# The eight turns of an attention kernel, written out in a row instead of six in a loop

## The chip, the cores and the metric

The kernel runs on one core of a Trainium2 chip. The metric is the device time of one launch in microseconds (us), as the median of several runs. A core has five engines with an instruction stream each: TensorE (PE in the profile, with its weight loads as PEld), VectorE (DVE), ScalarE (ACT), GpSimd (POOL) and SyncE (SP), which here only issues transfers. They meet through semaphores alone.

## The reference, cut to what matters

```python
x = L0_attn_x_bld                                  # (2, 2048, 256) float32
x = x + attention(layernorm(x))                    # 16 heads of 64, causal, keys and values from a 64-wide latent
x = x + ffn(layernorm(x))                          # 2 rounds: router, top 2 of 6 experts, shared experts, rms norm

# attention, per sequence b and head h
q = x @ Wq[:, h];  latent = x @ Wkv_down           # latent (2048, 64), shared by the heads
k = latent @ Wk_up[:, h];  v = latent @ Wv_up[:, h]
p = softmax(where(causal, q @ k.T / 8, -max))
y += (p @ v) @ Wout[h]
```

## The kernel before, in words

`build` first makes the combined weights, then runs `build_attention` for each of the two sequences in a loop over `b` that all engines execute (line 2238), and then `build_mixture`, the feed-forward part, which is written out in a row and is not touched.

`build_attention` works on pairs of heads: `PAIRS` is 8, and one pair is a **turn**. A turn has `2 * STEPS` = 80 steps, 40 for each head (called `half` in the code). A step is one block of scores: 128 keys (`kt`) against up to 512 queries (`qb`, four blocks of 512). Float32 precision is had by splitting each operand into a high and a low part. In one step:

- PE makes one block of scores of the next head, only to find its row maxima (`max_scores`, line 446), then the block of scores itself (lines 460 and 461), then the product of probabilities and values of five steps before (`use_latents`, lines 480 to 482, `LAG` = 5). Now and then it also projects queries of the next turn (line 426) and transposes a row of maxima (line 436).
- DVE masks a diagonal block (line 737, and 783 for the maxima), reads the maxima (line 786, `read_max`), splits queries (line 731), and at fixed steps inverts the sums of a finished block of queries (`invert`, line 742) and scales the result (`divide`, line 746). Three times per turn it makes a low part in POOL's place (line 363).
- ACT takes the exponential twice, as float32 (line 609, `pr`) and rounded (line 612, `ph`), and copies results out of PSUM (lines 570, 577, 588, 595).
- POOL makes the low parts `pl = pr - ph` (line 363), in a ring of `RING` = 8 buffers, and the low parts of the queries (line 675).
- SP moves the sums of a finished block to 128 partitions (line 379, `sums<-y_sums`), writes the reciprocals out (line 381), reads them back to 64 partitions (line 383) and stores the scaled block (line 388).

The order of the work is written out by hand in each engine's `turn`; no queue or planner chooses at run time. The last steps of a turn's products are done in the first steps of the next turn, so the turns overlap. DVE's `invert` for a block stands eleven steps behind the block's last score or less (`INVERT_AFTER` = 8) and in DVE's own order of instructions, so DVE waits there if the transfer of line 379 has not landed.

What the change touches is `turns` (line 315) and the end of SP's program (lines 407 to 411). Before, turn 0 and turn 7 are written out, and turns 1 to 6 are one body in a loop (`eng.Fori(1, PAIRS - 1)`, line 318) on PE, ACT, POOL and DVE. In that body `p` is a register, so that each wait's target value is computed by a register instruction (FUSED_REGOPS in the trace); in the written-out turns it is a constant. SP has two loops of its own, over turns 1 to 5 and over turns 6 and 7.

Of the kernel before, what the change touches and what calls it, by code (L numbers as in the profile page):

```python
# [38 lines left out]
PAIRS = H // 2  # L39
# [17 lines left out]
def f32(ap):  # L57
    return ap.bitcast(F32)
# [151 lines left out]
def build_attention(nc, T, x_seq, y_seq, recip_rows):  # L210
# [5 lines left out]
    with ExitStack() as ctx:  # L216
# [64 lines left out]
        def project_job(qb):  # L281

            return START_JOBS.index(("proj", qb))
# [30 lines left out]

        def turns(eng, turn):

            turn(0, True, False)
            with eng.Fori(1, PAIRS - 1) as p:
                turn(p, False, False)
            turn(PAIRS - 1, False, True)  # L320

        def block_jobs(job, s, after, p, first):

# [42 lines left out]
        with nc.Block() as block:  # L366
            @block.sync
            def _(sp):
                def stage(pair, projected):
                    if projected is not None:  # L370
                        sp.wait_ge(S["bank_made"], projected)
                    sp.dma_start(f32(stage_hi[:, :, :]), f32(T["m_hi"][:, pair, :, :])).then_inc(S["staged"], DMA)
                    sp.dma_start(f32(stage_lo[:, :, :]), f32(T["m_lo"][:, pair, :, :])).then_inc(S["staged"], DMA)

                def divide(p, half, qb):

                    n = 8 * p + 4 * half + qb
                    sp.wait_ge(S["y_copied"], n + 1)
                    sp.dma_start(sums[:, qb, :], y[LD:LD + 1, qb, :]).then_inc(S["sums_in"], DMA)
                    sp.wait_ge(S["recip"], n + 1)  # L380
                    sp.dma_start(recip_rows[qb], sums[:, qb, :]).then_inc(S["recip_out"], DMA)
                    sp.wait_ge(S["recip_out"], DMA * (n + 1))
                    sp.dma_start(rec[:, qb, :], recip_rows[qb:qb + 1, :, :].rearrange("a p j -> a (p j)").broadcast_to(
                        [LD, BLK])).then_inc(S["recip_in"], DMA)

                def store(p, half, qb):
                    sp.wait_ge(S["normed"], 8 * p + 4 * half + qb + 1)
                    sp.dma_start(y_seq[qb, half * LD:(half + 1) * LD, p, :], y[0:LD, qb, :]).then_inc(S[f"stored{qb}"], DMA)

                def turn(p, more, first=False):  # L390
                    for half in range(2):
                        for qb in range(QB):
                            divide(p, half, qb)
                            if half or qb:
                                store(p, half - (qb == 0), (qb - 1) % QB)
                            elif not first:
                                store(p - 1, 1, QB - 1)
                            if more and (half, qb) == (0, 2):
                                stage(p + 2, FIRST_JOBS + NJOBS * p + 8)

                for g in range(QB):
                    sp.dma_start(x[:, TPB * g:TPB * (g + 1), :],
                                 x_v[:, TPB * g:TPB * (g + 1), :]).then_inc(S[f"loaded{g}"], DMA)
                    if g == 0:
                        stage(0, None)
                stage(1, project_job(QB - 1) + 1)
                turn(0, True, first=True)
                with sp.Fori(1, PAIRS - 2) as p:
                    turn(p, True)
                with sp.Fori(PAIRS - 2, PAIRS) as p:  # L410
                    turn(p, False)
                store(PAIRS - 1, 1, QB - 1)
                for qb in range(QB):
                    sp.wait_ge(S[f"stored{qb}"], DMA * H)

            @block.tensor
            def _(pe):
# [67 lines left out]
                def turn(p, first, last):  # L485
                    for s in range(2 * STEPS):
                        half, m = s // STEPS, s % STEPS
                        if not (last and half == 1):
                            split_no = 8 * p + 4 * (half + 1) + MAX_STEPS[m][0] // TPB
                            max_scores(1 - half, m, split_no, STEPS + 2 * STEPS * p + s)  # L490
                        for n, (_, kind, head, qb) in jobs_at(s, last):
                            job = FIRST_JOBS + NJOBS * p + n
                            if kind == "row":
                                row(qb, 2 * p + head, job)
                            else:
                                project(p + 1, qb, job)
                        scores(half, m, s, p, first, last)
                        if s >= LAG:
                            use_latents(p, s - LAG)
                        elif not first:  # L500
                            use_latents(p - 1, 2 * STEPS + s - LAG)
# [54 lines left out]
                pe.wait_ge(S["k_lo"], QB)  # L556
                pe.wait_ge(S["filled"], 3)
                turns(pe, turn)
                for s in range(2 * STEPS - LAG, 2 * STEPS):
                    use_latents(PAIRS - 1, s)  # L560

            @block.scalar
            def _(act):
# [33 lines left out]
                def turn(p, first, last):  # L597
                    for s in range(2 * STEPS):
                        block_jobs(copy_sums, s, LAG + 1, p, first)
                        qb, kt = SCORE_STEPS[s % STEPS]  # L600
                        w = BLK - P * max(0, kt - TPB * qb)
                        if is_diagonal(s):
                            act.wait_ge(S["masked"], DIAGONALS * p + diagonals_before(s + 1))
                        else:
                            act.wait_ge(S["scored"], 2 * STEPS * p + s + 1)
                        src = ps[:, SCORE_BANK + s % 3, 0:w]
                        if not (first and s < RING):
                            wait_lo(act, p, s - RING)
                        act.activation(pr[:, s % RING, 0:w], src, ACT.Exp).then_inc(S["probs"], 1)  # L609
                        if not (first and s < RING):  # L610
                            act.wait_ge(S["latent_used"], 2 * STEPS * p + s - RING + 1)
                        act.activation(ph[:, s % RING, 0:w], src, ACT.Exp).then_inc(S["probs_hi"], 1)  # L612
                        for n, (_, kind, head, jqb) in jobs_at(s, last):
                            job = FIRST_JOBS + NJOBS * p + n
                            if kind == "row":
                                read_row(2 * p + head, head % 2, jqb, job)
                            else:
                                read_queries(p + 1, jqb, job)
                        for n, (_, head, jqb) in splits_at(s, last):
                            copy_queries(head % 2, jqb, *split_waits(p, head, jqb, first))  # L620
# [38 lines left out]
                for n in range(QB, FIRST_SPLITS):  # L659
                    copy_queries(1, n - QB, project_job(n - QB) + 1, None)  # L660
                turns(act, turn)
                late_jobs(copy_sums, LAG + 1)

            @block.gpsimd
            def _(pool):
# [53 lines left out]
                for n in range(QB, FIRST_SPLITS):  # L719
                    split_lo(1, n - QB, n)  # L720
                turns(pool, turn)

            @block.vector
# [1559 lines left out]
```

## Time and profile before

| what | us |
|---|---|
| median of 3 runs | 3055.87 (3052.61 to 3056.48) |
| the profiled execution: its own time | 3034.35 |
| its span, first to last instruction | 3032.4 |
| attention of the first sequence, turn 0 to turn 7 | from 106.5 to about 970 |
| attention of the second sequence, turn 0 to turn 7 | from 1062.1 to about 1925 |
| feed-forward part | from about 1945 to the end |
| PE busy over the span | 2701.1 (89%) |
| POOL, DVE, ACT busy over the span | 1940.6, 1930.6, 1719.7 |

The profile is one execution. "Busy" is the time in which an engine had an instruction in work; a row of a timeline gives start, duration, engine and line, and in brackets the idle time before it with what ended it ("issue" means that nothing that the profile shows was waited for). PEclk is the granted TensorE clock as a share of 2.4 GHz. Queue q8 and q14 carry instructions, q1 the transfers that SP issues.

### The profile page before, as it was taken

How to read it: one execution, taken by the hardware profiler on the slowest of the kernel's cores; microseconds unless marked ns; L12 is line 12 of the kernel's file. 1: busy time of each engine (PE TensorE's matmuls, PEld its weight loads, DVE VectorE, ACT ScalarE, POOL GpSimd, SP SyncE). 2: the span in 40 equal slices, each digit the busy share in tenths (PEclk: the TensorE clock that was granted, in tenths of full speed). 3: DMA queues.
4: the chain of work that ended last, by engine and by line, in shares of the span. 5: the costliest groups of instructions: out<-in, count | busy, mean ns of one | idle time of the engine just before them, and what ended most of it. 6: DMA issues, size and time to landing. Idle time of an engine off the chain costs nothing. (4 is left out here: it accounts for less than half of the span.)

```text
span 3032.4 us, 57352 instructions
## 1 busy us (share of the span) xinstructions
PE 2701.1 (89%) x13656; PEld 2244.8 (74%) x13656; DVE 1930.6 (64%) x4383; ACT 1719.7 (57%) x4016; POOL 1940.6 (64%) x1739
## 2 busy tenths in 40 slices
PE   5899999999998699999999999697874999879984
PEld 4687778878876378787787788586763888768873
DVE  4777777777783677777777776253633455664465
ACT  2577777777776277787777778432211443224442
POOL 2598889888897289888888889521340322463224
PEclk9799999999999699999999999898986999879997
DMA  3001101010011101010010010334432443224453
GB/s 67 10 23 26 25 19 25 22 22 22 19 26 24 36 17 22 23 25 19 22 29 22 19 22 21 105 126 136 139 127 88 148 144 101 77 101 132 154 163 120
DMA packets 165645, 186.93 MB, mean 62 GB/s; under 512 B 56941, under 2 KB 130931, under 8 KB 165369
## 3 DMA queue, kind: packets, MB, share of 16 engines
q1 hardware_dynamic: 152056, 150.17, 17.0%
q0 software_dynamic: 12288, 33.57, 3.4%
q14 instruction: 196, 1.60, 0.3%
q8 instruction: 81, 1.33, 0.2%
q10 hardware_dynamic: 1024, 0.26, 0.0%
HBM read 100.56 MB, written 78.64 MB: 59 GB/s over the span
## 5 line engine op out<-in xcount | busy, mean ns | idle before, releaser
L363 POOL TENSOR_TENSOR pl<-pr,ph 128x512 fp32r<-128x512 f32 (+3 forms) x1184 | 1374.1, 1185 | 199.5 <-ACT ph L612 169.0
L609 ACT ACTIVATE pr<-ps 128x512 f32<-128x512 f32 (+3 forms) x1280 | 692.6, 541 | 429.5 <-DVE ps L737 185.5
L786 DVE TENSOR_REDUCE part<-ps 128x1 f32<-128x512 f32 (+3 forms) x1152 | 705.4, 618 | 143.3 <-PE ps L446 123.6
L612 ACT ACTIVATE ph<-ps 128x512 fp32r<-128x512 f32 (+3 forms) x1280 | 692.8, 542 | 0.0
L446 PE MATMUL ps<-k_hi,q_parts 128*128 128x512 f32 (+3 forms) x1280 | 496.4, 390 | 50.7 <-DVE part L786 26.2
L460 PE MATMUL ps<-q_parts,k_hi 128*128 128x512 f32 (+3 forms) x1280 | 487.2, 381 | 0.3
L480 PE MATMUL ps<-ph,v_hi 128*128 128x512 f32 (+3 forms) x1280 | 476.2, 372 | 7.8 <-POOL pl L363 7.8
L461 PE MATMUL ps<-q_row,k_lo 65*128 65x512 f32 (+3 forms) x1280 | 474.2, 370 | 0.0
L481 PE MATMUL ps<-ph,v_lo 128*128 128x512 f32 (+3 forms) x1280 | 469.9, 367 | 0.0
L482 PE MATMUL ps<-pl,v_hi 128*128 128x512 f32 (+3 forms) x1280 | 467.1, 365 | 0.0
L446 PEld LDWEIGHTS ps<-k_hi,q_parts 128*128 128x128 f32 x1280 | 247.2, 193 | 138.7 <-DVE part L786 62.2
L480 PEld LDWEIGHTS ps<-ph,v_hi 128*128 128x128 f32 x1280 | 244.9, 191 | 61.0 <-POOL pl L363 16.1
L460 PEld LDWEIGHTS ps<-q_parts,k_hi 128*128 128x128 f32 x1280 | 243.6, 190 | 60.2 <-ACT ph L612 10.4
L481 PEld LDWEIGHTS ps<-ph,v_lo 128*128 128x128 f32 x1280 | 245.1, 191 | 38.0
L482 PEld LDWEIGHTS ps<-pl,v_hi 128*128 128x128 f32 x1280 | 242.5, 189 | 39.2
L461 PEld LDWEIGHTS ps<-q_row,k_lo 65*128 65x128 f32 x1280 | 244.4, 191 | 32.1
L1230 PE MATMUL ps<-xt,share_up 128*128 128x512 f32 x768 | 217.3, 443 | 56.6 <-DVE work L1876 51.5
L737 DVE TENSOR_TENSOR ps<-ps,mask_kq 128x128 f32<-128x128 f32 x512 | 149.9, 293 | 157.0 <-PE ps L461 124.9
L1631 POOL DMA_INDIRECT x_slots<-xcur,slot_i x128 | 125.3, 979 | 184.1 <-PE ps L1351 82.5
L1230 PEld LDWEIGHTS ps<-xt,share_up 128*128 128x128 f32 x768 | 161.3, 215 | 100.0 <-DVE work L1876 55.8
L1351 PE MATMUL ps<-exp_up,yy 128*128 x888 | 234.0, 399 | 0.0
L675 POOL TENSOR_TENSOR q_parts<-q_raw,q_parts 64x512 fp32r<-64x512 f32 x128 | 175.4, 1370 | 78.6 <-DVE q_parts L731 61.4
(207 smaller groups left out, 3834.0 us busy)
## 6 DMA issues: line engine op xcount, KB each, us to landing
work<-x_slots SPq DMA_DIRECT2D x148, 128.0 KB, 2.4
e_slots<-work SPq DMA_DIRECT2D x148, 128.0 KB, 1.9
rec<-recip_rows SPq DMA_DIRECT2D x128, 128.0 KB, 3.4
y_latent<-y_sums SPq DMA_DIRECT2D x128, 128.0 KB, 2.9
yg<-y_latent SPq DMA_DIRECT2D x32, 512.0 KB, 5.4
x_slots<-accr SPq DMA_DIRECT2D x8, 1184.0 KB
acc_shared<-accw SPq DMA_DIRECT2D x14, 512.0 KB, 8.6
accr<-acc_shared SPq DMA_DIRECT2D x14, 512.0 KB, 4.6
```

The source lines that it names most:

```text
L363: eng.tensor_tensor(pl[:, s % RING, 0:w], pr[:, s % RING, 0:w], f32(ph[:, s % RING, 0:w]), ALU.subtract).then_inc(sem, 1)
L446: pe.matmul(ps[:, MAX_BANK + m % 2, 0:w], qa[half][:, i * P:(i + 1) * P], kh[:, c * BLK:c * BLK + w], start=True, stop=True).then_inc(S["m ...
L460: pe.matmul(out, kh[:, k], qa[half][:, q], start=True, stop=False)
L461: pe.matmul(out, kl[0:LD + 1, k], qc[half][:, q], start=False, stop=True).then_inc(S["scored"], 1)
L480: pe.matmul(out, va[:, kt, :], ph[:, b, 0:w], start=kt == 0, stop=False)
L481: pe.matmul(out, vc[:, kt, :], ph[:, b, 0:w], start=False, stop=False)
L482: pe.matmul(out, va[:, kt, :], pl[:, b, 0:w], start=False, stop=kt == TPB * (qb + 1) - 1).then_inc(S["latent_used"], 1)
L609: act.activation(pr[:, s % RING, 0:w], src, ACT.Exp).then_inc(S["probs"], 1)
L612: act.activation(ph[:, s % RING, 0:w], src, ACT.Exp).then_inc(S["probs_hi"], 1)
L786: ins = dve.tensor_reduce(dst, src[:, 0:w], AX.X, ALU.max)
L1230: mm = pe.matmul(out, sup[:, a, kind, n, dt, m * P:(m + 1) * P], xt[:, x, dt, :], start=i == 0, stop=i == len(terms) - 1)
L1351: mm = pe.matmul(out, tx[:, t % 2, x, dt, :], wu[:, b, bass.ds(expert[t], 1), dt, :], start=False, stop=n == len(terms) - 1)
```

## The change

The bodies of the turns stay as they are. All eight are emitted one after another, with `p` a constant in each, on all five engines; the loop over the two sequences stays.

```diff
         def turns(eng, turn):
 
-            turn(0, True, False)
-            with eng.Fori(1, PAIRS - 1) as p:
-                turn(p, False, False)
-            turn(PAIRS - 1, False, True)
+            for p in range(PAIRS):
+                turn(p, p == 0, p == PAIRS - 1)
...
                 stage(1, project_job(QB - 1) + 1)
-                turn(0, True, first=True)
-                with sp.Fori(1, PAIRS - 2) as p:
-                    turn(p, True)
-                with sp.Fori(PAIRS - 2, PAIRS) as p:
-                    turn(p, False)
+                for p in range(PAIRS):
+                    turn(p, p < PAIRS - 2, first=p == 0)
                 store(PAIRS - 1, 1, QB - 1)
```

## Rows read from the trace of the kernel before

**Rows 1.** The page's busy time: us, share of the span, instructions.

```profile
PE 2701.1 (89%) x13656; PEld 2244.8 (74%) x13656; DVE 1930.6 (64%) x4383; ACT 1719.7 (57%) x4016; POOL 1940.6 (64%) x1739
```

**Rows 2.** Windows: length, busy of PE, PEld, DVE, ACT, POOL; PEclk, DMA share, GB/s.

```profile
439.69:549.64 109.95, 106.69 (x512) 87.50 (x512) 81.56 (x181) 83.38 (x188) 97.62 (x82) 1.00 0.10 23
2360.00:2480.00 120.00, 120.00 (x748) 107.16 (x747) 52.31 (x132) 55.74 (x174) 38.10 (x40) 1.00 0.45 142
```

**Rows 3.** Timeline of ACT: first exponentials of turns and half turns.

```profile
164.45 0.60 ACT L609 ACTIVATE pr<-ps 128x512 f32<-128x512 f32 x1 [0.91 <-DVE ps L737]
...
216.40 0.60 ACT L609 ACTIVATE pr<-ps 128x512 f32<-128x512 f32 x1 [1.11 <-POOL pl L363]
...
272.16 0.60 ACT L609 ACTIVATE pr<-ps 128x512 f32<-128x512 f32 x1 [1.02 <-DVE ps L737]
...
329.37 0.60 ACT L609 ACTIVATE pr<-ps 128x512 f32<-128x512 f32 x1 [4.18 <-DVE ps L737]
...
439.69 0.60 ACT L609 ACTIVATE pr<-ps 128x512 f32<-128x512 f32 x1 [3.94 <-DVE ps L737]
...
494.94 0.60 ACT L609 ACTIVATE pr<-ps 128x512 f32<-128x512 f32 x1 [1.02 <-POOL pl L363]
...
549.64 0.60 ACT L609 ACTIVATE pr<-ps 128x512 f32<-128x512 f32 x1 [3.90 <-DVE ps L737]
...
825.75 0.60 ACT L609 ACTIVATE pr<-ps 128x512 f32<-128x512 f32 x1 [1.02 <-POOL pl L363]
...
877.68 0.60 ACT L609 ACTIVATE pr<-ps 128x512 f32<-128x512 f32 x1 [1.03 <-DVE ps L737]
...
1173.39 0.60 ACT L609 ACTIVATE pr<-ps 128x512 f32<-128x512 f32 x1 [1.10 <-POOL pl L363]
...
1229.13 0.60 ACT L609 ACTIVATE pr<-ps 128x512 f32<-128x512 f32 x1 [1.02 <-DVE ps L737]
...
1285.15 0.60 ACT L609 ACTIVATE pr<-ps 128x512 f32<-128x512 f32 x1 [3.91 <-DVE ps L737]
...
1833.90 0.60 ACT L609 ACTIVATE pr<-ps 128x512 f32<-128x512 f32 x1 [1.03 <-DVE ps L737]
```

**Rows 4.** Waits of DVE, 110 to 970 (us, times, longest), and its timeline.

```profile
DVE ps L737 <- issue: 14.4, 5, 3.1
...
328.94 0.30 DVE L737 TENSOR_TENSOR ps<-ps,mask_kq 128x128 f32<-128x128 f32 x1 [3.09 <-issue]
```

**Rows 5.** Timeline of PE behind the start of turn 2.

```profile
329.84 0.44 PE L446 MATMUL ps<-k_hi,q_parts 128*128 128x384 f32 x1 [2.17 <-DVE mx L786]
```

**Rows 6.** Branches by line: count, ns min/median/max, first and last start.

```profile
L318 DVEq COMPARE_BRANCH  x12: 55/63/63, 325.8 to 1833.5; - x12
...
L2238 PEldq COMPARE_BRANCH  x2: 83/2138/4193, 988.2 to 1943.6; - x2
```

**Rows 7.** Windows as in rows 2: two stretches of lower clock.

```profile
551.30:554.60 3.30, 3.30 (x15) 2.91 (x14) 2.41 (x6) 1.77 (x7) 2.98 (x4) 0.50 0.00 1
291.90:295.20 3.30, 3.30 (x13) 2.82 (x12) 3.21 (x5) 1.46 (x3) 2.69 (x4) 0.50 0.29 75
```

**Rows 8.** Timeline of SP's queue and DVE around three transfers of line 379.

```profile
284.47 0.51 SPq L379 DMA_DIRECT2D sums<-y_sums  x1
...
288.26 0.18 DVE L742 RECIPROCAL sums<-sums 128x4 f32<-128x4 f32 x1 [1.78 <-DMA sums<-y_sums]
...
398.86 0.18 DVE L742 RECIPROCAL sums<-sums 128x4 f32<-128x4 f32 x1
...
1245.45 0.18 DVE L742 RECIPROCAL sums<-sums 128x4 f32<-128x4 f32 x1 [2.05 <-DMA sums<-y_sums]
```

**Rows 9.** Code queues (packets, MB, share): 106.5 to 216.4, 285 to 288.5, 329.4 to 770.

```profile
q8 instruction: 4, 0.07, 0.3%
...
q8 instruction: 1, 0.02, 1.7%
...
q14 instruction: 44, 0.36, 0.5%
```

## The prediction

> **What bounds the kernel now.** I read the page first. PE is busy 89% of the span, the others 57% to 64% [rows 1], so in the attention the question is what keeps PE from its next matmul. Next I cut the attention into turns. ACT's first exponential of a turn is a good mark, because its start follows from all engines; the marks of turn 1, turn 7 and the half turns between are in [rows 3]. A turn of the loop takes 549.64 - 439.69 = 109.95 us [rows 3], PE is busy 106.69 of it with 512 matmuls, and POOL, the next, 97.62 [rows 2]. So PE sets the pace, with about 3 us per turn to be had from it and about 12 us of room on POOL.
>
> Then I looked for where those 3 us lie. The waits of DVE hold one that nothing in the profile releases: 5 times in the first sequence, 14.4 us in all, before the first mask of a turn (line 737) [rows 4]. Five is the number of times that the loop of line 318 goes back (turns 1 to 5 end in a jump; turn 6 falls out of it). The row at 328.94 has 3.09 us of idle before it [rows 4]. ACT, which waits for this mask, is idle for 4.18, 3.94 and 3.90 us at the marks of turns 2, 3 and 4, but for 1.03 at 877.68, the start of turn 7, where nothing jumps back [rows 3]. PE runs into it two steps later: it waits 2.17 us for DVE's maxima at 329.84 [rows 5]. So the jump costs DVE 2.8 to 3.1 us, and PE some 2 us of standing still plus what it takes to fill the pipeline again. The second sequence has the same. That is the whole of what the change can remove at the edges: ten jumps back.
>
> **The change part by part.** *The jumps.* I price them from marks, not from PE's idle alone, since a stop is partly made up for afterwards and partly made worse.
> A turn without a stop at either end isn't in the loop, but its halves are in the trace. Entered without a stop, a first half takes 272.16 - 216.40 = 55.76 us, and in the second sequence 1229.13 - 1173.39 = 55.74 [rows 3]; entered behind a stop it takes 494.94 - 439.69 = 55.25 [rows 3], because the stop has let the others catch up. A second half with no jump behind it (turn 6) takes 877.68 - 825.75 = 51.93; with the jump (turn 3) 549.64 - 494.94 = 54.70 [rows 3]. So a jump costs 54.70 - 51.93 = 2.77 us, of which the next turn gives back 0.5: 2.3 us net. A written-out turn should take 55.75 + 51.93 = 107.7 us.
> Turns 1 to 6 took 877.68 - 216.40 = 661.3 us in the first sequence and 1833.90 - 1173.39 = 660.5 in the second [rows 3]. Six turns of 107.7 are 646.1. The gain is 15.2 + 14.4 = 29.6 us. Ten jumps of 2.3 make 23 of it; the rest is the two things that follow.
>
> *The clock.* The granted clock stands at 1.00, that is 2.4 GHz, but falls to 0.50 (1.2 GHz) for 3.3 us right behind the jump at 549 and behind a stop in turn 1 [rows 7]. PE had just stood still both times. Such a stretch can cost at most half its length, 1.6 us. These costs are inside the 29.6, since the marks hold them, and should go with the stops.
>
> *The register instructions.* In the loop, each engine computes the values of its waits; written out, they are constants. I cost that at nothing. The work that hides it is PE's matmul stream: the instructions go through sequencers that run ahead of the engines. The marks compare the two directly: the second half of turn 0, written out, takes 216.40 - 164.45 = 51.95 us, that of turn 6, in the loop, 51.93 [rows 3]. If that cover were gone it would be a gain, not a loss: PE's idle in a turn is 109.95 - 106.69 = 3.3 us [rows 2], nearly all of it the stop, so I allow 0.25 us for each of 12 turns. Bound: 0 to 3 us.
>
> *SP.* Its loops lie in other places than the compute engines' (behind turn 5 and over 6 and 7), and nothing waits for them; it issues the same transfers in the same order. Zero.
>
> *The code itself.* Here lies the cost. Written out, PE has to be sent its instructions for every turn; as a loop, it was sent the body once. Queue q8 carries 4 blocks in turn 0; from 329.4 to 770, turns 2 to 5, the answer lists q14 alone as carrying instructions, with 44 small packets, and no q8 [rows 9]. Such a block gets in the way of small transfers. DVE's reciprocal of the fifth block of a turn stands close behind the transfer of line 379: in turn 2 it runs at once at 398.86, but in turn 1, issued at 284.47, DVE waits 1.78 us for it until 288.26, and one q8 block went over in just this stretch [rows 8, 9]. In the second sequence's turn 1 the same instruction waits 2.05 us [rows 8]. The second half of those turns then takes 329.37 - 272.16 = 57.21 and 1285.15 - 1229.13 = 56.02 us against 54.70 [rows 3]: 2.5 us, with a clock stretch in it, and 1.3 us. What is late next is DVE's reading of maxima, and for that PE.
> How often will that meet in the new turns? With some 4 blocks per 108 us against a transfer open for 3.8 us at most (284.47 to 288.26 [rows 8]), chance alone gives 4 x 3.8 / 108, one turn in seven, so 2 of the 12; the two turns 1 had it 2 times out of 2, so all 12 at worst. The blocks come by PE's count of instructions, which doesn't divide into turns, so the meeting should wander. I take 3 of 12 at 1.5 us: 4.5 us. The bounds are 0 and 12 x 1.3 = 15.8 us.
>
> The Trainium skill, "Runtime: NRT & Kernel Launch", section "Instruction fetch mechanics", says that the cost of passing a block boundary is mostly hidden; by that rule the last term would be 0 and the sum 29.6. For PE itself the rows agree, for a small transfer beside it they don't.
>
> **The sum.** 29.6 - 4.5 = 25 us. The profiled execution had 3034.35 us, its span 3032.4; it would become 3009. The median of the runs is 3055.87, 21.5 us above it, and I have no row for this difference, so I take the same 25 us off: 3031. The bounds of the terms give 29.6 + 3 = 33 at best and 29.6 - 15.8 = 14 at worst, so 3023 to 3042.
>
> **The rivals.**
> *The jump is cheap and the change does nothing.* The branch instruction on DVE has a median of 63 ns [rows 6]; ten of them are 0.6 us, which gives 3055. Against it: the row behind it is 3 us late, only there, and not where the branch isn't taken [rows 4]. The Trainium skill, "Advanced Engine Details and Errata", section "Control Flow Timing", has about 108 ns for a compare-and-branch; by that, ten would be about 1 us, an estimate from that page, and the change would not be measurable. The trace bears this out for the instruction but not for what comes behind it. Chance 0.03.
> *PE has to wait for its code (the other side).* A jump of PE that isn't held took up to 4193 ns, at line 2238 [rows 6]. Turns 2 to 6 of both sequences need some 40 blocks that were not sent before (10 turns of 4 [rows 9]). If each held PE as long, that is 168 us and the time is 3056 + 168 - 30 = 3194. It decides from 29.6 / 40 = 0.7 us per block: above that the kernel gets slower. Against it: first halves of turn 1 with blocks on q8 are as long in both sequences, 55.76 and 55.74, and in the feed-forward part, written out, PE is busy 120.00 of 120.00 us, with more matmuls per us (748) than here [rows 2]. Chance 0.04.
> *The meeting with the transfer happens in most turns.* 9 or more of the 12 at 1.3 to 2.5 us: a gain of 7 to 18, 3038 to 3049. For it: 2 of 2 in turns 1. Against it: the drift. Chance 0.12.
> *The register instructions held something back,* and turns get faster than 107.7: a gain over 33, 3020 or below. Against it: the halves of 51.95 and 51.93 us, written out and in the loop [rows 3]. Chance 0.04.
>
> **How the numbers follow.** My forecast (gain 14 to 33) has the remaining 0.77. Its time is 3031. Range for 8 in 10: 3020 to 3044, which takes in a part of the third rival and some spread between chips. 0.2% is 6 us, about what a measurement of this kernel can tell from no change. Faster: 0.77 + 0.04 and nearly all of the 0.12, so 0.92. Same: 0.03 plus a little of the third rival, 0.04. Slower: 0.04.
>
> **What would show it.** The wait of line 737 for "issue" is gone in the new profile, and so is the 2 us idle of PE behind a turn's start. Marks of turns 1 to 6 are 107.7 us apart, some of them 1.3 to 2.5 more, and in just these the reciprocal of line 742 waits for its transfer. Queue q8 has some 40 packets more than before. No clock stretch of 0.50 at a turn's start. The prediction is wrong if turns without a stop take 109 us or more (then something else than the jump paced them), if PE shows waits that nothing releases (its code is late), or if the reciprocal waits in every turn.

## The result, and the profile after

| | us |
|---|---|
| changed kernel, median of 7 | 3035.42 (3029.66 to 3044.53) |
| kernel before, 7 runs beside them | 3056.48 (3050.79 to 3059.07) |
| ratio, 95% interval | 0.9934 (0.9919 to 0.9950) |
| profiled execution of the changed kernel | 3038.84, span 3037.1 |

The change makes the kernel 0.66% faster (0.50 to 0.81), which is 20 us; 25 were forecast. The two profiled executions say nothing of this if one compares their spans, 3032.4 and 3037.1. The feed-forward part, which nobody touched, took 1107 us from the attention's last exponential to the end in the one and 1127 in the other. In the later runs it took 1101 to 1114 us where the kernel before had a median of 3029 to 3034, and 1126 to 1131 where it had 3052 to 3055. What makes this difference is open. It goes with the group of runs and not with the chip's number, since e1 to e4 and e9 and e10 are all recorded on chip 1. So the attention must be compared by its own marks.

The marks, ACT's first exponentials of turns 1, 2 and 3, of turn 7, and of turns 1 and 7 of the second sequence, in the timeline of the changed kernel:

```profile
220.15 0.60 ACT L604 ACTIVATE pr<-ps 128x512 f32<-128x512 f32 x1 [0.91 <-DVE ps L732]
...
328.02 0.60 ACT L604 ACTIVATE pr<-ps 128x512 f32<-128x512 f32 x1 [0.89 <-DVE ps L732]
...
437.12 0.60 ACT L604 ACTIVATE pr<-ps 128x512 f32<-128x512 f32 x1 [0.89 <-DVE ps L732]
...
869.64 0.60 ACT L604 ACTIVATE pr<-ps 128x512 f32<-128x512 f32 x1 [0.91 <-DVE ps L732]
...
1169.07 0.60 ACT L604 ACTIVATE pr<-ps 128x512 f32<-128x512 f32 x1 [0.89 <-DVE ps L732]
...
1818.13 0.60 ACT L604 ACTIVATE pr<-ps 128x512 f32<-128x512 f32 x1 [0.89 <-DVE ps L732]
```

ACT's idle ahead of them is 0.9 us where it was 3.9 to 4.2 [rows 3]. The six turns take 869.64 - 220.15 = 649.5 us and 1818.13 - 1169.07 = 649.1, against 661.3 and 660.5: 23.2 us less. The waits of DVE over the six turns of the first sequence are now these (us, times, longest), with no wait for "issue" of line 732, which answers to line 737 [rows 4]:

```profile
DVE ps L732 <- PE ps L456: 40.5, 82, 1.0
DVE part L781 <- PE ps L441: 36.7, 57, 1.7
DVE ps L778 <- PE ps L441: 24.5, 31, 2.0
DVE y_sums L741 <- DMA rec<-recip_rows: 7.6, 12, 1.6
DVE q_parts L726 <- ACT q_raw L565: 4.5, 12, 0.4
DVE pl L361 <- ACT ph L607: 4.3, 11, 0.5
DVE sums L737 <- DMA sums<-y_sums: 1.6, 3, 0.7
```

The window of these six turns (length, busy of PE, PEld, DVE, ACT, POOL, PEclk, DMA share, GB/s), after and then before:

```profile
220.15:869.64 649.49, 639.27 (x3074) 523.35 (x3073) 517.31 (x1081) 501.85 (x1128) 581.34 (x493) 1.00 0.09 23
```

```profile
216.40:877.68 661.28, 643.79 (x3074) 527.43 (x3073) 498.76 (x1081) 501.35 (x1128) 582.20 (x491) 0.99 0.10 22
```

PE's idle fell from 661.28 - 643.79 = 17.5 us to 649.49 - 639.27 = 10.2, and the clock stays at 1.00. But DVE, with the same 1081 operations, is busy 18.6 us longer. That was not forecast. All of it lies in the 36 low parts that DVE makes in POOL's place (line 361, before line 363). Here they are by themselves, in the same window, after and then before:

```profile
220.15:869.64 649.49, 49.12 (x36) 1.00 0.09 23
```

```profile
216.40:877.68 661.28, 30.25 (x36) 0.99 0.10 22
```

Runs e5 to e8 are about this. The page's queues of instructions q8 and q14 (packets, MB, share of 16 engines) went from 81 and 196 packets to

```profile
q8 instruction: 123, 2.02, 0.3%
q14 instruction: 137, 1.12, 0.1%
```

### The profile page after: what moved, and what is told of

Read it like the earlier page. It is cut to its first block and busy times, and to the rows that moved or that the text cites. A ratio compares the mean times of both kernels' runs of the same rounds, so it can differ in the third digit from the quotient of the medians.

```text
span 3037.1 us, 47786 instructions
## 1 busy us (share of the span) xinstructions
PE 2704.6 (89%) x13656; PEld 2243.3 (74%) x13656; DVE 1969.8 (65%) x4383; ACT 1721.8 (57%) x4016; POOL 1935.6 (64%) x1739
```

## The experiments

Twelve kernels. "Six turns" is the measure from above, for both sequences; "steps 20 to 30" is ACT's time from the first exponential of step 20 to that of step 30 of turn 2. Times are ratios to the kernel before, run beside them on the same chip. e1 to e4 ran together (median of the kernel before there 3033.7), and so did e5 to e8 (3029.2), e9 and e10 (3055.0), and e11 and e12 (3051.8).

| kernel | six turns | steps 20 to 30 | ratio (95%) |
|---|---|---|---|
| before | 661.3, 660.5 | 14.5 | 1 |
| changed | 649.5, 649.1 | 15.3 | 0.9934 (0.9919 to 0.9950) |
| e1 DVE in its loop | 673.5, 681.8 | 15.4 | 1.0093 (1.0068 to 1.0118) |
| e2 ACT in its loop | 647.8, 646.7 | 14.5 | 0.9927 (0.9903 to 0.9951) |
| e3 PE and POOL in their loops | 642.8, 642.9 | 14.5 | 0.9892 (0.9873 to 0.9912) |
| e4 loops of before, told where they jump | 645.0, 645.6 | 14.5 | 0.9894 (0.9874 to 0.9914) |
| e5 changed kernel again | 648.3, 647.4 | 15.3 | 0.9934 (0.9918 to 0.9950) |
| e6 POOL in its loop | 643.0, 642.1 | 14.5 | 0.9902 (0.9881 to 0.9922) |
| e7 PE in its loop | 650.2, 649.8 | 15.3 | 0.9942 (0.9920 to 0.9963) |
| e8 changed, step 20's low part on POOL | 640.7, 644.4 | 14.5 | 0.9883 (0.9859 to 0.9906) |
| e9 two turns in the loop's body | 669.8, 672.7 | 14.6 | 1.0087 (1.0069 to 1.0104) |
| e10 e3, later reciprocals | 647.3, 647.5 | 14.5 | 0.9927 (0.9911 to 0.9943) |
| e11 e4 with e8 | 647.5, 647.7 | 14.5 | 0.9925 (0.9903 to 0.9946) |
| e12 e7 with e8 | 646.1, 645.8 | 14.5 | 0.9922 (0.9899 to 0.9945) |

**Whose jump is it? e1, e2, e3.** Each takes the changed kernel and keeps the loop over turns 1 to 6 on some engines:

```diff
-            for p in range(PAIRS):
-                turn(p, p == 0, p == PAIRS - 1)
+            turn(0, True, False)
+            if eng is nc.vector:              # e2: nc.scalar; e3: nc.tensor or nc.gpsimd
+                with eng.Fori(1, PAIRS - 1) as p:
+                    turn(p, False, False)
+            else:
+                for p in range(1, PAIRS - 1):
+                    turn(p, False, False)
+            turn(PAIRS - 1, False, True)
```

> The change, but VectorE keeps its loop over turns 1 to 6. The measure is the six turns: from ScalarE's first exponential of turn 1 to that of turn 7, 661.3 and 660.5 us in the kernel before, 649.5 and 649.1 in the changed one. Theory (VectorE's jump back is what stops the pipeline, because its code comes late): the stops of 2.8 to 3.1 us stay, six turns take 658 to 663 us, the gain in time is 5 us or less. Rival 1 (the register instructions on the other engines held the turns back): six turns near 650, gain near 20. Rival 2 (ScalarE's own jump, 2.5 us long, costs as much): about halfway, near 655.

> The change, but ScalarE alone keeps its loop. In the kernel before, ScalarE branches at 324.93, goes on at 327.56, and then still waits for VectorE's mask until 329.37; with VectorE on time the first exponential comes 1.25 us behind the branch (876.43 to 877.68), so ScalarE's 2.5 us of standing stick out by 1.3 us. Theory: five stops of about 1.0 to 1.3 us per sequence, six turns 654 to 656 us, gain 8 to 14 us. Rival 1 (VectorE's jump alone counts): six turns near 649, gain near 21. Rival 2 (any engine's late code costs the full 2.3): 660, gain near 0.

> The change, but TensorE and GpSimd keep their loops, whose jumps take 0.2 us; VectorE, ScalarE and SyncE are written out. Theory (stops come from VectorE's and ScalarE's code, register instructions cost nothing, and TensorE's code blocks delay the transfer of the sums): no stop, no 16 KB code block in turns 2 to 6, the reciprocal never waits there, six turns of 107.3 to 107.9 us, 644 to 648 us, gain 23 to 28 us. Rival 1 (TensorE's 385 register instructions per turn hold it): six turns over 652. Rival 2 (the blocks don't delay that transfer, something else does): some turns still 0.5 to 1.3 us longer, 649 as in the changed kernel.

e1 has the stops back, as the waits of DVE in its first sequence show:

```profile
DVE ps L738 <- issue: 14.5, 5, 3.0
```

That is the whole of the stop before [rows 4], so VectorE's jump makes it, and rival 1 is out. But e1 is not equal to the kernel before, as the theory had it: it is 0.93% slower. The stops are the same; the turns between them are longer. Steps 10 to 20 take 14.5 us where they took 13.5, and steps 20 to 30 take 15.4 where they took 14.5. In both, VectorE's low part is slow. This is the one of step 10 of turn 2, before and in e1:

```profile
344.57 0.42 DVE L363 TENSOR_TENSOR pl<-pr,ph 128x256 fp32r<-128x256 f32 x1
```

```profile
345.95 1.51 DVE L367 TENSOR_TENSOR pl<-pr,ph 128x256 fp32r<-128x256 f32 x1
```

These two stretches make 11 of the 12 us that the first sequence lost. The second sequence lost 21; it also has five stretches of 3.4 to 6.9 us at a granted clock of 0.50, and the first has one.

e2 was forecast at 654 to 656 us and came out at 647.8 and 646.7, less than the changed kernel. Its gain of 0.73% is that of rival 1. But ScalarE's jump is not free in it. Steps 70 to 80 take 14.0 to 14.9 us in the turns that end in a jump and 12.6 in turn 6, which ends in none; the first ten steps of the next turn give back 0.8 (13.1 us against 13.9 in turn 1). My estimate from these marks is some 0.8 us per jump. It is hidden in the total because steps 20 to 30 are back at 14.5.

e3 came out better than forecast: no stop, no code block on q8 in turns 2 to 6, 642.8 us with 385 register instructions per turn left on PE. e6, below, has none of them on PE and takes 643.0 and 642.1, so they cost PE nothing there. One forecast of e3 failed: the reciprocal still waits for its transfer, 5 times and 0.9 us at most in turns 2 to 6 of the first sequence, though no block is left there.

**Is it the fetch of the code? e4.** The kernel before, with its loops, where VectorE and ScalarE get an instruction at the loop's top that names the jump at its end:

```diff
+            ahead = eng is nc.vector or eng is nc.scalar
-            with eng.Fori(1, PAIRS - 1) as p:
+            with nc.Fori(1, PAIRS - 1, engines=bass.OrderedEngineSet([eng.engine]), hint_back_edge=ahead) as p:
                 turn(p, False, False)
```

The timeline of DVE at the start of turn 2 of e4:

```profile
327.53 0.17 DVE L793 TENSOR_REDUCE mx<-part 128x4 f32<-128x16 f32 x1
328.12 0.30 DVE L738 TENSOR_TENSOR ps<-ps,mask_kq 128x128 f32<-128x128 f32 x1 [0.42 <-issue]
```

The stop is 0.42 us and not 3.09 [rows 4]: the same branch, in the same loop. So it was the code at the loop's top that came late, and this is the experiment that shows it. A loop that is told ahead is worth 1.06% (0.86 to 1.26), more than writing the turns out (0.50 to 0.81).

**The changed kernel again, and the 0.8 us in steps 20 to 30. e5, e6, e7, e8.** e5 is the changed kernel unaltered; e6 and e7 are as e1 with `nc.gpsimd` and `nc.tensor`; e8 is

```diff
-ON_DVE = [s % STEPS in (10, 20, 30) for s in range(2 * STEPS)]
+ON_DVE = [s % STEPS in (10, 30) for s in range(2 * STEPS)]
```

> The changed kernel itself, once more, beside the three that follow. All theories: six turns of 649 to 650 us in each sequence, as in its first profile; steps 20 to 30 of a turn 15.3 us; gain about 20 us. What it tells apart is whether those numbers belong to the program or to the one execution: if steps 20 to 30 take 14.5 us here in some turns, the theory of a fixed phase falls.

> The changed kernel, but GpSimd alone keeps its loop (its jump takes 0.3 us), so it has register instructions between its operations again. Theory (VectorE's operation from memory to memory in step 20 lasts until GpSimd's running operation ends, 1.8 us where 1.0 would do, and it is GpSimd's pauses that let it in): step 20's operation takes below 1.2 us, steps 20 to 30 take 14.5 us, a turn without other trouble 107.1 to 107.4 us, six turns 644 to 647 us. Transfers of the sums with a 16 KB code block in flight still take 2.5 us or more. Rival (GpSimd's pauses have nothing to do with it, the order of TensorE's or ScalarE's waits has): steps 20 to 30 stay at 15.3 us and six turns at 649.

> The changed kernel, but TensorE alone keeps its loop, so that no 16 KB code block goes over queue q8 in turns 2 to 6. Theory (every transfer of the sums that is slower than 2.5 us in the changed kernel was met by such a block): no slow transfer of the sums with a q8 block beside it behind turn 1, turns of 107.88 us without the 0.5 to 0.8 us extras, six turns 647 to 648.5 us with steps 20 to 30 still at 15.3 us, gain about 1.5 us over the changed kernel. Rival (the register instructions on TensorE cost time where nothing else slows it): six turns above 650. Rival (TensorE's loop, not GpSimd's, is what made steps 20 to 30 short in the run before): steps 20 to 30 at 14.5 us and six turns near 643.

> The changed kernel, but the low part of step 20 is made by GpSimd and not by VectorE (2 instead of 3 steps per head on VectorE, the same result). Theory (the 1.8 us of VectorE's operation in step 20 is what makes steps 20 to 30 0.8 us longer than in the loop): steps 20 to 30 take 14.5 us, and with GpSimd's busy time up by some 2.4 us per turn, to about 100 of 107, six turns take 644 to 648 us. Rival (TensorE is paced there by something else): 15.3 us stays. Rival (GpSimd becomes the bound): steps 20 to 40 longer than now, six turns above 650.

Here are DVE's low part of step 20 in turn 2 and, behind it, POOL's operations around it, one by one. First the kernel before, then the changed one, e6 and e2:

```profile
357.93 0.98 DVE L363 TENSOR_TENSOR pl<-pr,ph 128x512 fp32r<-128x512 f32 x1
...
357.07 1.29 POOL L363 TENSOR_TENSOR pl<-pr,ph 128x512 fp32r<-128x512 f32 x1 [0.25 <-POOL q_parts L675]
358.32 1.74 POOL L363 TENSOR_TENSOR pl<-pr,ph 128x512 fp32r<-128x512 f32 x1
```

```profile
356.63 1.81 DVE L361 TENSOR_TENSOR pl<-pr,ph 128x512 fp32r<-128x512 f32 x1
...
355.35 1.29 POOL L361 TENSOR_TENSOR pl<-pr,ph 128x512 fp32r<-128x512 f32 x1
356.60 1.29 POOL L361 TENSOR_TENSOR pl<-pr,ph 128x512 fp32r<-128x512 f32 x1
```

```profile
355.01 0.91 DVE L367 TENSOR_TENSOR pl<-pr,ph 128x512 fp32r<-128x512 f32 x1
...
355.33 1.74 POOL L367 TENSOR_TENSOR pl<-pr,ph 128x512 fp32r<-128x512 f32 x1
```

```profile
357.12 0.68 DVE L367 TENSOR_TENSOR pl<-pr,ph 128x512 fp32r<-128x512 f32 x1
...
355.93 1.29 POOL L367 TENSOR_TENSOR pl<-pr,ph 128x512 fp32r<-128x512 f32 x1
357.18 1.77 POOL L367 TENSOR_TENSOR pl<-pr,ph 128x512 fp32r<-128x512 f32 x1
```

One operation of the same shape takes 0.98, 1.81, 0.91 and 0.68 us. The rows show what decides: which engine comes first when POOL starts its next operation. In the kernel before, DVE's starts 0.39 us ahead of POOL's next one; DVE's takes 0.98, and POOL's takes 1.74 us where it otherwise takes 1.29. In the changed kernel POOL's is 0.03 us ahead; it takes its 1.29, and DVE's lasts until that one has ended, and then some 0.5 us more. The Trainium skill, "SBUF — State Buffer", section "SBUF: two separate sides", says that VectorE's operations with two inputs in that memory and GpSimd's take turns at a shared port pair, held for a whole instruction; the rows agree.

e6 gives POOL its loop back, and with it register instructions and short pauses between its operations, like the 0.25 us above. POOL comes later, steps 20 to 30 take 14.5 us and the six turns 643.0 and 642.1. So POOL's loop is enough. But its pauses don't let DVE in by themselves, as I had expected, and they are not needed: in e2 POOL is written out and has no pause there, DVE is 0.06 us ahead of it, and steps 20 to 30 take 14.5 too. What a pause does is to shift one engine against the other. e8 takes the one operation away from DVE: 14.5 us too, and with 0.9883 the lowest ratio of all. e7, with PE alone in its loop, keeps 15.3, so it is not PE's waits. TensorE does not pace these steps, then, and GpSimd did not become the bound: both rivals of e8 are out. One forecast of e6 failed: of its 17 transfers of the sums that were met by a q8 block, ten took 2.4 us or less.

e5 shows that this belongs to the program: 15.3 us again, plain turns of 107.88 us again. But e7 missed: no code blocks in turns 2 to 6, and still 650.2 and 649.8 us. It has extras of 0.4 to 0.8 us over 107.9 in turns 1, 4, 5 and 6 of both sequences; they lie in steps 50 to 60, which take 13.2 to 14.1 us there and 11.8 in turns 2 and 3. So extras come without blocks too; what makes these is open. Nor can e7 rule out its first rival, a cost of PE's register instructions, set at above 650 us; against it stands e3, which has them too and is as fast as e6.

**Fewer jumps instead of none. e9.**

```diff
-            with eng.Fori(1, PAIRS - 1) as p:
-                turn(p, False, False)
+            with eng.Fori(0, (PAIRS - 2) // 2) as r:
+                turn(2 * r + 1, False, False)
+                turn(2 * r + 2, False, False)
```

> The kernel before with two turns in the body of the loop of TensorE, ScalarE, VectorE and GpSimd: three passes, two jumps back per sequence instead of five. Theory (each jump back costs 2.3 us net): six jumps fewer in all, 14 us less, six turns 653 to 656 us (before: 661.3 and 660.5), at the ends of turns 2 and 4 alone VectorE stands for 2.8 us. TensorE's body, 2800 instructions, is now longer than what it kept before: if its jump then waits for its code, up to 4.2 us as at line 2238, the stops are longer and q8 carries blocks in every turn; then six turns 656 to 662. Rival (the loop's cost is spread over the turns and not at the jumps): no difference between turns with and without a jump, six turns near 661.

Slower than before, by 0.87%, with two jumps per sequence instead of five. The branches of line 318 (count, ns min/median/max) and the waits of PE (us, times, longest) from 215 to 890:

```profile
L318 PEldq COMPARE_BRANCH  x6: 82/3559/3654, 437.8 to 1853.4; - x6
```

```profile
PE ps L447 <- issue: 6.1, 2, 3.1
```

PE's jump, which took 0.2 us when the body was one turn, takes 3.6 us, and queue q8 carries 26 blocks from 330 to 770 where it had none. So I take it that the body no longer fits in what PE keeps. That is only half of what went wrong. The first sequence's six turns take 27 us more than six turns like turn 6 of the kernel before (107.14 us); turns 2 and 4, which end in a jump, hold 13.6 of it, and the four without one hold 13.4 (110.8 us for turn 3). Their steps 10 to 20 take 15.2 us and not 13.5, and VectorE's low part of step 10 takes 1.52 us there, as in e1. So it looks like POOL and DVE once more; no run has tested this.

**Better versions. e10, e11, e12.** e10 is e3 with `INVERT_AFTER` 9 and `DIVIDE_AFTER` 14; e11 is e4 with e8's edit; e12 is e7 with e8's edit.

> The best so far (TensorE and GpSimd in their loops, VectorE and ScalarE written out: six turns of 642.8 us, 1.08% faster than before), with VectorE's reciprocal and division each one step later (9 and 14 instead of 8 and 13). In the best so far the reciprocal of a turn's fifth block waited 0.2 to 1.5 us for its transfer in each turn. Theory (that wait delays TensorE): the waits go, six turns 640 to 642.5 us, gain 33 to 37 us. Rival (the wait was covered by TensorE's own work): no difference beyond 1 us. Rival (the moved operations meet GpSimd's in worse places): six turns above 644.

> Two edits that each won put together, on the loops of the kernel before: VectorE and ScalarE are told at the loop's top where it will jump back to (alone: six turns of 645, gain 1.06%), and GpSimd makes the low part of step 20 (alone, on the written-out turns: six turns of 640.7 and 644.4, gain 1.17%). If the two causes are independent, the turns lose the 0.8 us only where step 20 cost it; in the loop step 20 took 1.0 us and not 1.8, so there is less to win: six turns 641 to 645 us, gain 31 to 37 us. Rival (GpSimd, which has register instructions here, becomes the bound with one operation more): six turns above 647.

> The written-out turns with GpSimd making the low part of step 20, and TensorE alone in its loop, so that no 16 KB code block goes over queue q8 in turns 2 to 6. The run without TensorE's loop had a plain turn of 106.5 us and extras of 1.5 to 2.6 us in 5 of 12 turns. Theory (most extras came from transfers met by code blocks): extras mostly gone, six turns 639 to 641.5 us, gain 36 to 40 us. Rival (the extras are VectorE's operations meeting GpSimd's, whatever queue q8 carries, as in the run with TensorE alone in its loop, 650 instead of the 648 expected): six turns 641 to 646, as without TensorE's loop.

e10 and e11 are worse than what they were built from: 647 us against 642.8, and 647.5 against 645. e12, at 646, is better than e7 (650) and worse than e8 (640.7 and 644.4). In e10 the reciprocal still waits, up to 1.7 us, and its third expectation, six turns above 644, came true; that the whole chain had moved is my guess. In e11 and e12 steps 20 to 30 are 14.5 as wanted, and the time is lost again in other steps: 70 to 80 in e11 (14.2 us, 13.2 in e4), 50 to 60 in e12 (13.2 to 14.1 in eight of the twelve turns, 11.8 or 11.9 in the others). Both lie at their rivals' values. Two edits that each won alone did not add up.

## Why the prediction was right

The time, the direction and the range held: 20 us of 25, 3035.42 in 3020 to 3044. The main mechanism, the jumps, held too. That the sum came so near is in part luck, since terms of up to 13 us cancel in it.

*The jumps.* Shown, by e1 (VectorE's loop alone brings the stops back) and e4 (told ahead, the stop falls to 0.42 us). The written-out turn was put together from two halves as 107.7 us; the plain ones measure 107.88 (turn 1: 328.02 - 220.15). Two errors partly cancel in it: its first half is 0.36 us longer than the forecast 55.75, with 0.8 more in steps 20 to 30 and less elsewhere, and its second half is 0.15 shorter than 51.93.

*The clock.* As forecast, no stretch of 0.50 in the changed six turns of either sequence.

*The register instructions.* Zero for PE, as forecast (e3 against e6; by e7 against e5 it could be up to 2.5 us per sequence). The step "if that cover were gone it would be a gain, not a loss" failed for POOL: without these instructions its operations come earlier against DVE's, and that costs 0.8 us per turn in steps 20 to 30, 10.5 to 13.5 us over both sequences as e6 has it (1296 to 1299 us for the twelve turns changed, 1285 in e6). It did not show in the total because the turn without a stop was forecast too long as well: in e6 it takes 107.0 us and not 107.7, which makes 8 us over twelve turns. That these two nearly cancel is luck. Half turns of turn 0 held this in plain sight: its steps 20 to 30 took 15.3 us in the kernel before, and I had compared second halves only.

*The code blocks.* Mis-sized in its parts; the sum came out near by luck. The extras over 107.88 come to 1298.6 - 12 x 107.88 = 4.0 us in the first profile and 1.1 in e5, for 4.5 forecast. In the first profile a transfer of the sums that a q8 block met was indeed slow. Here is one of turn 3 in the second sequence, in the changed kernel, with its row of the transfers' view (count, KB, median us to landing) and of the queues from 1454 to 1457:

```profile
1453.78 0.51 SPq L377 DMA_DIRECT2D sums<-y_sums  x1
...
1457.08 0.18 DVE L737 RECIPROCAL sums<-sums 128x4 f32<-128x4 f32 x1 [0.49 <-DMA sums<-y_sums]
```

```profile
q8 instruction: 1, 0.02, 2.0%
...
sums<-y_sums SPq DMA_DIRECT2D x1, 2.0 KB, 3.3
```

3.3 us against a median of 2.0. Eight of the 128 transfers were met like this, all took 2.5 to 3.5 us, and they cost their turns 0 to 0.8 us, not 1.3 to 2.5. I take it that DVE, which needs more time in the written-out turns, arrives later and has less to wait for; this is not shown. But a q8 block is neither needed nor enough. Three transfers that met none took 2.8 to 2.9 us, beside some 260 KB of other transfers. In e5 seven met one and four of these took 2.0 us. Of the 4.0 us of extras, 1.7 (1.2 in turn 2 and 0.5 in turn 5 of the first sequence) had no block that met such a transfer, and in e5 the turns with the extras had none either. So no run here shows the 4.5 us as a cost of the blocks; what the runs show for them is 0 to 2.3 us.

*SP.* "Zero" was wrong, and this term takes some 4 us off the 23 won in the turns. The last store of the first sequence and the first load of the second, in SP's queue, before and then after:

```profile
982.20 0.50 SPq L388 DMA_DIRECT2D y_latent<-y_sums  x1
988.60 0.42 SPq L402 DMA_DIRECT2D pr<-in_x  x1
```

```profile
974.91 0.50 SPq L386 DMA_DIRECT2D y_latent<-y_sums  x1
985.75 0.41 SPq L400 DMA_DIRECT2D pr<-in_x  x1
```

6.4 us have become 10.8. They lie behind SP's own branch at the end of the loop over the sequences. These are its branch there (first start) and the instruction behind it (last start), before and then after:

```profile
L2238 SPq COMPARE_BRANCH  x2: 40/45/50, 988.1 to 1943.5; - x2
...
L2238 SPq MOVE  x3: 38/41/46, 36.1 to 988.4; - x3
```

```profile
L2233 SPq COMPARE_BRANCH  x2: 49/54/59, 981.2 to 1929.6; - x2
...
L2233 SPq MOVE  x3: 38/46/46, 36.3 to 985.5; - x3
```

0.3 us have become 4.3. The first exponential of the second sequence comes 73.5 us behind this load in both kernels (at 1062.12 and 1059.25), so the whole sequence starts as much later. All fourteen kernels fall into two groups by this: in the four that keep SP's loops (before, e4, e9, e11) the two rows of SP's queue are 6.4 us apart, in the ten that have SP written out 9.6 to 10.8. That SP's code comes late there, as VectorE's did, is likely from the place of the stop, but no run told this loop ahead.

23.2 us won in the turns less 4.4 lost here is 18.8, and 20 were measured. For e3, which has SP written out, it is 36.1 less about 4, measured 33; for e4, with nothing to take off, 31.2, measured 32. No kernel differs in SP's loops alone, so that the stop costs the whole 4.4 us rests on the comparison of these runs.

*The 21.5 us between the profiled execution and the median,* for which I had no row, fit the feed-forward part, which took some 20 us more in some groups of runs than in others, as the section on the result has it. There is no profile of the kernel before at some 3055 us, so this is not shown.

*The rivals.* The cheap jump is out: the branch takes 63 ns [rows 6] and what comes behind it 3 us, gone when the code is fetched ahead. PE waiting for its code did not happen in written-out turns: PE has no wait for "issue" there. It happened in e9, through a jump, and made half of what e9 lost.

*Slips in the working.* The worst case of the code blocks is 12 x 1.3 = 15.6 us and not 15.8, and the third rival's gain of 7 to 18 us holds for 9 turns; with all 12 at 2.5 us there would be no gain left. Neither moves the forecast.

## What to carry to other kernels

A jump back can cost what the code at its target costs to fetch. That is to be read engine by engine, since here it was 0.2 us on one and 3 on the next, and a longer body made it worse on each: look in the waits for "issue" ahead of a turn's first instruction, and try telling the loop ahead before writing it out, which here won 32 us where writing out won 20. A longer body with fewer jumps can be worse than a short one with many. Look at the engine that only issues transfers too; here it gave back 4 us of 23. And where two engines share a way to memory, removing instructions that look like overhead can shift them by a few hundredths of a microsecond into each other's way: compare the duration of one operation of the same shape in both kernels before calling anything free.

## What the runs showed of the hardware

- A jump back over a body of about 384 instructions on VectorE took 2.8 to 3.1 us from the branch to the next instruction, over about 510 on ScalarE 2.5 to 2.6, over 1410 on TensorE and 256 on GpSimd 0.2 to 0.3 (kernel before). With twice the body (e9) TensorE's took 3.6 us and GpSimd's 0.6. Told ahead: 0.24 us on VectorE and 0.45 on ScalarE (e4).
- The loop over the sequences cost SyncE 0.3 us at its jump with its inner loops kept, and 3.0 to 4.3 us with its program written out.
- One VectorE operation of 128x512 with both inputs in SBUF, that of step 20, took 0.68 us (e2) to 1.82 (changed kernel), by whether GpSimd's next one started 0.06 us behind it or 0.03 ahead of it; at this step it was the same in turns 1 to 6 of a kernel within 0.04 us. The one that came second took longer: GpSimd's 1.77 us and not 1.29.
- A 2 KB transfer took 2.0 us as a rule. Beside a 16 KB block of TensorE's code it took 2.5 to 3.5 us in eight of eight cases in the changed kernel, and 2.0 us in four of seven in the same kernel's other profile (e5).
